# A mixture-of-experts, two-attention and quantised-FFN kernel: 39 whole expert tiles against 25 whole and 11 of two 64-row units

## What is computed

```python
gate = rmsnorm(x) @ wg_W + wg_b + (cond @ gg_W + gg_b)         # 8 experts
cw   = top-2 of softmax(gate), the other six zero
h1   = relu(x @ W1[e] + b1[e])                                 # 256 -> 512
h2   = relu(h1 @ W2[e] + b2[e])                                # 512 -> 512
m    = sum over e of cw[e] * (h2 @ W3[e] + b3[e])              # 512 -> 256
q, k, v = tanh(m @ W + b)                                      # 16 heads of 64
x1   = x + tanh(softmax_causal(q k^T / 8) v @ Wo + bo)
a    = attention of 16 heads of 16 on x1, its shares scaled by a gate and mixed with a field share
out  = x1 + quant(a) @ quant(ffn_weight)^T + bias              # blocks of 32, FP4 steps
```

## Time and profile before

| | us |
|---|---|
| median of three runs | 797.6 |
| the profiled execution, its own time | 797.88 |
| its span, first to last instruction | 796.0 |
| TensorE matmuls busy | 754.4 |
| VectorE busy | 497.0 |
| ScalarE busy | 279.1 |
| GpSimd busy | 81.4 |

### The profile page before, as it was taken

How to read it: one execution, slowest core, us unless ns; L and a number is a source line. 1 busy time by engine, 2 the same in 40 slices (tenths; PEclk the granted TensorE clock), 3 DMA queues, 4 the chain that set the end, 5 groups by cost and what they waited for, 6 DMA issues and landing times.

```text
span 796.0 us, 23085 instructions
## 1 busy us (share of the span) xinstructions
PE 754.4 (95%) x9468; PEld 656.8 (83%) x9468; DVE 497.0 (62%) x1090; ACT 279.1 (35%) x838; POOL 81.4 (10%) x91
## 2 busy tenths in 40 slices
PE   5489999999999999989999999999999999999786
PEld 2389989999999999967778878977897789778675
DVE  4764574443444454235688778777877787778756
ACT  3032112112212211244446435633563455336420
POOL 2221111111111100010000000000000000000000
PEclk9599999999999999999999999999999999999989
DMA  9788243111111112300000000010000000000000
GB/s 320 277 268 275 90 163 123 35 34 42 34 34 42 39 30 81 99 28 21 22 22 9 28 28 16 16 29 28 9 22 29 28 9 21 28 9 15 9 9 15
DMA packets 29686, 48.53 MB, mean 61 GB/s; under 512 B 3307, under 2 KB 19435, under 8 KB 29069
## 3 DMA queue, kind: packets, MB, share of 16 engines
q1 hardware_dynamic: 20432, 32.47, 12.0%
q0 software_dynamic: 3408, 9.31, 4.1%
q10 hardware_dynamic: 5741, 5.27, 2.0%
HBM read 39.82 MB, written 7.22 MB: 59 GB/s over the span
## 4 chain that ended last, share of the span: by engine, by line
PE 89%; DVE 7%; ACT 1%; issue 1%; another core or an unknown queue 1%; POOL 1%; DVEq 0%; ACTq 0%; POOLq 0%
PE ps L621 17%; PE ps L696 15%; PE ps L610 8%; PE ps L633 8%; PE ps L775 7%; PE ps L721 7%; PE ps L743 4%; PE ps L795 3%; PE ps L766 2%; PE ps L736 2%; PE ps L826 2%; PE ps L807 2%; PE ps L873 2%; PE ps L841 2%; PE ps L890 2%; PE ps L863 1%
## 5 line engine op out<-in xcount | busy, mean ns | idle before, releaser
L621 PE MATMUL ps<-h_t,w_now 128*128 128x128 f32 x1248 | 145.9, 275 | 1.0 <-DVE h_t L1362 1.0
L621 PEld LDWEIGHTS ps<-h_t,w_now 128*128 128x128 f32 x1248 | 142.4, 192 | 1.5 <-issue 1.4
L696 PE MATMUL ps<-arena,l_weights 128*128 128x128 f32 x1024 | 127.5, 279 | 3.0 <-ACT arena L1044 3.0
L696 PEld LDWEIGHTS ps<-arena,l_weights 128*128 128x128 f32 x1024 | 121.0, 194 | 4.3 <-ACT arena L1044 3.2
L1006 ACT ACTIVATE h_t<-ps,cols 128x128 f32<-128x128 f32 x156 | 44.5, 368 | 215.0 <-PE ps L610 193.7
L1353 DVE COPY w_now<-arena 128x2048 f32 x39 | 47.9, 1227 | 105.7 <-PE ps L621 98.8
L1050 ACT ACTIVATE arena<-ps,cols 128x128 f32<-128x128 f32 x256 | 73.1, 371 | 20.9 <-PE ps L696 20.9
L610 PEld LDWEIGHTS ps<-xg_t,w_now 128*128 128x128 f32 x624 | 75.3, 192 | 4.8 <-DVE w_now L1345 2.1
L610 PE MATMUL ps<-xg_t,w_now 128*128 128x128 f32 x624 | 76.4, 276 | 2.3 <-ACT xg_t L997 2.0
L633 PE MATMUL ps<-arena,h_t 128*128 x312 | 73.8, 379 | 0.0
L505 POOL DMA_INDIRECT xg<-in_x,slot_tok x39 | 45.7, 1173 | 232.8 <-PE ps L600 203.8
(11 more groups left out here) (245 smaller groups left out, 1011.9 us busy)
## 6 DMA issues: line engine op xcount, KB each, us to landing
arena<-in_w SPq DMA_DIRECT2D x16, 512.0 KB
arena<-in_w SPq DMA_DIRECT2D x8, 1024.0 KB
expert_out<-y ACTq DMA_DIRECT2D x39, 128.0 KB
arena<-in_x_t SPq DMA_DIRECT2D x2, 1024.0 KB, 6.4
arena<-in_x SPq DMA_DIRECT2D x16, 128.0 KB, 2.8
out<-arena SPq DMA_DIRECT2D x16, 128.0 KB, 1.7
b<-in_b SPq DMA_DIRECT2D x1, 1024.0 KB, 12.8
l_weights<-in_wq SPq DMA_DIRECT2D x1, 1024.0 KB
```

What stands on the lines that cost most here:

```text
L621: last = mm(ps[:, 2, m * P:(m + 1) * P], w2_now[:, k, m * P:(m + 1) * P], h1_t[j % 2][:, k, :], start=k == 0, stop=k == KM - 1)
L696: last = mm(ps[:, b, c * P:(c + 1) * P], wt[:, k, f:f + P], m_t[:, k, :], start=k == 0, stop=k == KH - 1)
```

## The change

- The 4096 rows are cut in 25 whole tiles of one expert and 11 **mixed** tiles of two units of 64 rows, each unit with an expert of its own: each expert's rows fill whole tiles as far as they go, and what is left goes into units. 36 tiles in all. The mixed ones run as positions 13 to 23 (FIRST_MIXED, LAST_MIXED).
- In a mixed tile the tokens are the stationary side (64 wide), one column half of TensorE for each unit, and the unit's W1, W2 or W3 streams 512 or 256 columns. The rows come out unturned: VectorE adds the bias rows (add_b1, add_b2; gathered by GpSimd, one row for each slot), TensorE turns them (turn_h1, turn_h2, four transposes each), ScalarE applies the ReLU. W1 and W2 are copied for both units (VectorE), W3 too (take_w3, ScalarE), which stands ahead of the store of y, now one step later than before in a mixed step.
- take_w1 and take_w2 wait for TensorE before they read the register, in all tiles.
- The dispatch computes three segments for each expert (first whole tile, other whole tiles, rest in units); independent instructions go out without a wait (step.go).
- The quantising of the FFN weight is spread over side stages j = 4 to 10, its transposes are at j = 8.
- SP loads the attention weights after layer 3 of position 23, since the second copies of the weights lie in that space.
- The values of token tile 0 lie in banks 1 and 2: l1_v(0) waits for no activation, the scores for the keys alone; keep_busy(12) is put behind l1_turn_m(1). VectorE mixes tile 1 before it adds the second half of tile 0's bias.

The diff, cut:

```diff
-SLOT_TILES = (TOPK * TOK + EXP * (P - 1)) // P
+UNIT = 64
+UNITS = P // UNIT
+FULL = -(-(TOPK * TOK - EXP * (P - 1)) // P)
+MIXED = -(-(TOPK * TOK - FULL * P + EXP * (UNIT - 1) - (UNIT - 1)) // P)
+SLOT_TILES = FULL + MIXED
 LAST = SLOT_TILES - 1
+FIRST_MIXED = EXP + 5
+LAST_MIXED = FIRST_MIXED + MIXED - 1
+BIAS_BUFS = 2
 H1, D1 = 16, 64
...
+def value_bank(t, s):
+
+    return (1, 2)[s] if t == 0 else (3, 0)[s]
...
+def mixed(p):
+
+    return FIRST_MIXED <= p <= LAST_MIXED
...
+def nth(p):
+
+    return p - FIRST_MIXED if mixed(p) else p if p < FIRST_MIXED else p - MIXED
...
+def slot_tile(p):
+
+    return FULL + nth(p) if mixed(p) else nth(p)
...
+    def go(self, instruction):
+        instruction.then_inc(self.sem, 1)
+        self.n += 1
...
+            sp.wait_ge(y_ps, LAST_MIXED + 1)
...
+                if mixed(j - 2):
+                    n = nth(j - 2)
+                    if n == 0:
+                        pool.wait_ge(row_expert_set, 1)
+                        pool.wait_ge(setup_done, 1)
+                        pool.wait_ge(fa_stored, 16)
+                    if n >= BIAS_BUFS:
+                        pool.wait_ge(h1r_set, n - BIAS_BUFS + 1)
+                    pool.indirect_dma_start(
+                        out=b1_rows[n % BIAS_BUFS], out_offset=None, in_=t_in["b1"],
+                        in_offset=bass.IndirectOffsetOnAxis(ap=row_expert[:, n:n + 1], axis=0)).then_inc(b1_gathered[n % BIAS_BUFS], 16)
...
-                    pool.wait_ge(y_stored, 16 * EXP)
+                    pool.wait_ge(y_stored, 16 * (LAST_MIXED + 1))
...
             def layer1(j):
-                pe.wait_ge(w1_set, j + 1)
                 pe.wait_ge(xt_set, j + 1)
                 if j:
-                    pe.wait_ge(h1t_set, j)
+                    if mixed(j - 1):
+                        pe.wait_ge(h1r_set, nth(j - 1) + 1)
+                    else:
+                        pe.wait_ge(h1t_set, j)
+                pe.wait_ge(w1_set, j + 1)
+                if mixed(j):
+                    for k in range(KH):
+                        for g in range(UNITS):
+                            part_ = slice(g * UNIT, (g + 1) * UNIT)
+                            last = mm(ps[part_, 0, :], xg_t[:, k, part_], w1_of[g][:, k, :],
+                                      start=k == 0, stop=k == KH - 1, tile_position=(0, g * UNIT))
+                    last.then_inc(l1_ps, 1)
+                    return
...
+            def turn_h1(j):
+                pe.wait_ge(h1r_set, nth(j) + 1)
+                if nth(j):
+                    pe.wait_ge(h1t_set, j)
+                for m in range(KM):
+                    last = pe.transpose(ps[:, 1, m * P:(m + 1) * P], h1_rows[:, m * P:(m + 1) * P], ident[:, :])
+                last.then_inc(h1r_turned, 1)
...
+                if mixed(j):
+                    pe.wait_ge(h2m_set, nth(j) + 1)
+                    pe.wait_ge(y_set, j)
+                    pe.wait_ge(w3_set, nth(j) + 1)
+                    for k in range(KM):
+                        for g in range(UNITS):
+                            part_ = slice(g * UNIT, (g + 1) * UNIT)
+                            last = mm(ps[part_, 4, 0:HID], h2_t[j % 2][:, k, part_], w3_now[g][:, k, :],
+                                      start=k == 0, stop=k == KM - 1, tile_position=(0, g * UNIT))
+                    last.then_inc(y_ps, 1)
...
                     layer1(j + 1)
                 if exists(j + 2, SLOT_TILES):
                     turn_x(j + 2)
+                if mixed(j - 1):
+                    turn_h2(j - 1)
                 if exists(j, SLOT_TILES):
                     layer2(j)
+                if mixed(j + 1):
+                    turn_h1(j + 1)
                 if exists(j - 1, SLOT_TILES):
                     layer3(j - 1)
 
...
-                if j == 7:
+                if j == 8:
...
-                pe.wait_ge(qk_set, 4 * t + 3 + s)
+                if t:
+                    pe.wait_ge(qk_set, 4 * t + 3 + s)
...
-                pe.wait_ge(vb_set, 2 * t + 2)
+                if t:
+                    pe.wait_ge(vb_set, 2 * t + 2)
+                else:
+                    pe.wait_ge(qk_set, 4)
...
             l1_turn_m(1)
+            keep_busy(12)
             l1_q(1, 0)
...
+            def relu2_mixed(j):
+                act.wait_ge(h2r_turned, nth(j) + 1)
+                act.wait_ge(y_ps, j - 1)
+                f(h2_t[j % 2][:, :, :], ps[:, 3, :].rearrange("p (k q) -> p k q", k=KM), ACT.Relu).then_inc(h2m_set, 1)
+
+            def take_w3(j):
+                if nth(j) == 0:
+                    act.wait_ge(setup_done, 1)
+                    act.wait_ge(fa_stored, 16)
+                    act.wait_ge(moe_loaded, 48 * EXP)
+                act.wait_ge(y_ps, j)
+                for g in range(UNITS):
+                    e = act.value_load(row_expert[g * UNIT:g * UNIT + 1, nth(j):nth(j) + 1], min_val=0, max_val=EXP - 1)
+                    at = act.snap(e * E_SIZE + W3_AT)
+                    last = act.copy(w3_now[g].rearrange("p k n -> p (k n)"), arena[:, bass.ds(at, KM * HID)])
+                last.then_inc(w3_set, 1)
...
+                if mixed(j - 1):
+                    take_w3(j - 1)
+                    if exists(j + 2, SLOT_TILES):
+                        copy_x(j + 2)
+                    relu2_mixed(j - 1)
+                    store_y(j - 2)
+                    if exists(j + 1, SLOT_TILES):
+                        relu1(j + 1)
+                else:
+                    if exists(j + 1, SLOT_TILES) and not mixed(j + 1):
+                        relu1(j + 1)
+                    if exists(j + 2, SLOT_TILES):
+                        copy_x(j + 2)
+                    if mixed(j + 1):
+                        relu1(j + 1)
+                if exists(j - 1, SLOT_TILES) and not mixed(j):
...
-            step(ts(first_slot, iota_m8, float(EXP), float(P), ALU.add, ALU.mult))
-            step(dve.memset(first_expert, 0.0))
-            step(ts(first_expert[:, 0:EXP], iota_m8[:, 0, :], float(EXP), None, ALU.add))
...
+            step.go(ts(full_i, count_i, -P, None, ALU.bitwise_and))
+            step(ts(up_i, count_i, float(UNIT - 1), None, ALU.add))
+            step.go(ts(seg_of[0], full_i, float(P), None, ALU.min))
+            step(ts(up_i, up_i, -UNIT, None, ALU.bitwise_and))
+            step.go(tt(seg_of[1], full_i, seg_of[0], ALU.subtract))
+            step(tt(seg_of[2], up_i, full_i, ALU.subtract))
+            step.go(dve.tensor_tensor_scan(seg_ends, seg, scan_zero.rearrange("p e i -> p (e i)")[:, 0:3 * EXP], 0.0, ALU.add, ALU.add))
+            step.go(tt(past_full, full_i, first_row, ALU.add))
...
             def take_w1(j):
+                if j:
+                    dve.wait_ge(l1_ps, j)
+                if mixed(j):
+                    if nth(j) == 0:
+                        dve.wait_ge(setup_done, 1)
+                        dve.wait_ge(fa_stored, 16)
+                        dve.wait_ge(moe_loaded, 48 * EXP)
+                    experts_of[j] = [unit_expert(j, g) for g in range(UNITS)]
+                    for g in range(UNITS):
+                        at = dve.snap(experts_of[j][g] * E_SIZE + W1_AT)
+                        last = dve.tensor_copy(w1_of[g][:, :, :].rearrange("p k n -> p (k n)"), arena[:, bass.ds(at, KH * MID)])
+                    last.then_inc(w1_set, 1)
+                    return
...
+            def take_w2(j):
                 if j:
-                    dve.wait_ge(l1_ps, j)
-                dve.tensor_copy(w1_now[:, :, :].rearrange("p k n -> p (k n)"), arena[:, bass.ds(at, KH * MID)]).then_inc(w1_set, 1)
-
-            def take_w2(j):
+                    dve.wait_ge(l2_ps, j)
+                if mixed(j):
+                    for g in range(UNITS):
+                        at = dve.snap(experts_of[j][g] * E_SIZE + W2_AT)
+                        last = dve.tensor_copy(w2_of[g][:, :, :].rearrange("p k n -> p (k n)"), arena[:, bass.ds(at, KM * MID)])
+                    last.then_inc(w2_set, 1)
...
+            def add_b1(j):
+                n = nth(j)
+                dve.wait_ge(l1_ps, j + 1)
+                dve.wait_ge(b1_gathered[n % BIAS_BUFS], 16 * (n // BIAS_BUFS + 1))
+                if n:
+                    dve.wait_ge(h1r_turned, n)
+                tt(h1_rows, bank(0), b1_rows[n % BIAS_BUFS], ALU.add).then_inc(h1r_set, 1)
...
+                if mixed(j + 1):
+                    add_b1(j + 1)
                 if exists(j + 2, SLOT_TILES):
                     take_w1(j + 2)
                 if j == LAST - 1:
                     l1_mix(0)
+                if mixed(j):
...
+                if j == 5:
+                    step(stt(xb(two(w_tmp)), xb(two(w_raw)), 1.0, bc(two(w_inv), BLK), ALU.mult, ALU.mult))
+                    step(ts(w_tmp, w_tmp, FP4_MAX, -FP4_MAX, ALU.min, ALU.max))
+                    step(ts(w_mag.bitcast(I32), w_tmp.bitcast(I32), EXPONENT, None, ALU.bitwise_and))
+                if j == 6:
```

(13 more changed lines are left out.)

225 lines of the change are left out of this document (158 added, 67 removed).

## The result

The changed kernel takes **787.65 us** (median of five runs, 786.08 to 789.31), the kernel before 797.6 (of its five runs beside them four lie between 795.66 and 798.33, one took 2634.36): ratio 0.987, 95% interval 0.985 to 0.989. The prediction was 789.0 us in a range of 782.0 to 796.5.

A forecast was written before the change was run, and what follows sets the result against it. TensorE, busy 95% of the span, bounds the kernel. Against the profiled 797.88 us: -21.9 + 13.8 + 1.0 + 1.0 + 1.2 - 1.6 - 0.9 - 1.4 = -8.8, giving 789.1, stated as 789.0 us; range 782 to 796.5.

The forecast's parts named there:

- Tiles out and mixed tiles in: Expert tiles: three steady steps fewer, -21.9 us; eleven mixed steps of 8.56 us, 1.26 above a full one, +13.8 us.
- Overlap and switching: Mixed-tile products: halves overlap at 0.427 us a pair pass; each visit to the 64-wide form costs about 0.31 us extra.
- (c): Mixed step: halves do not overlap because the stationary sides differ too; 15.4 us a step, 864 us in all; chance 4%.
- (d): Mixed steps: no switching cost and an early start of everything; 782 us in all; chance 10%.
- VectorE in the mixed step: VectorE's work, busy about 6.1 of 8.56 us, put at nothing while the mixed step stays above about 6.6 us.
- rival (b): Slower than before: VectorE bounds the mixed step, needing 9.6 us with all reads exposed; 801 us; chance 8%.
- Register reads: take_w1, take_w2: copies begin about 0.85 us later; 0.04 a full tile, +1.0 us, and first two tiles +1.0 us.
- rival (a): Full tiles: the register read becomes their bound, 0.3 us a tile, +7 instead of +1, 795 us; chance 12%.
- Dispatch: Path to the first x gather: new chain +2.0, three instructions gone -0.6, smaller tables -0.1; +1.2 us (0.5 to 2).
- Quantising: Tiles of 95.71 to 119.65: pieces hidden in VectorE's idle time remove TensorE's wait at L663; -1.6 us.
- The banks, the clock: Token tile 0: free banks start scores earlier, -0.9 us; keep_busy(12) shortens the idle piece, keeping the clock up, -1.4 us.

## Why the prediction was right

**Tiles out and mixed tiles in.** The step of 8.56 us came out as 8.57, eleven of them 13.9 above full tiles. The whole stretch costs 15.3 (124.88 us from the turn_x at 129.50 to that at 254.38, less 15 x 7.305): 13.9 are the eleven steps, 0.63 is the stall at the entry, the other 0.8 the edges, where a step has both forms (7.59, 8.63, 8.13 at the entry, 8.63, 7.95, 8.09 at the end). On the third chip, without the stall, it is 14.7. Neither was in the sum: VectorE and GpSimd had been put at nothing, and the edges were not looked at.

**Overlap and switching.** Both confirmed by their own runs: overlap whole only by alternation (11.25 us without it), 0.30 us a visit. Rivals (c) and (d) fall. The ground for (c), that the halves keep apart when the stationary sides differ too, is not borne out: they differ in every mixed step, and it takes 8.57 us. What costs overlap is the order of the products, and even with the halves in turn the step is 11.25 and the time 816, not 15.4 and 864.

**VectorE in the mixed step**, rival (b), needs 6.91 us, against 6.6 in the prediction and 9.6 in the rival; there were 1.66 us to spare.

**Register reads.** +1.0 at the start: 0.74. +1.0 for full tiles: nothing, and the whole of rival (a) with it. Slack and delay had been reckoned equal to 0.01, but the delay was mis-sized: 0.66 us in the full tiles, not 0.85, which leaves 0.31 ahead of the next layer 2. The 0.87 goes from the start of one copy to the start of the next, and 0.69 of it is the W1 copy itself. Full tiles stand 7.30 or 7.31 us apart with the read behind the wait as with the read ahead of it.

**Dispatch.** Predicted +1.2, made of +2.0 for the chain, -0.6 for three instructions and -0.1 for the tables. The chain took 6.78 us from 22.48 to 29.26 instead of 5.52: +1.26. The three instructions were 0.63 (17.23 to 17.86 in the trace of before) and the tables give 0.10, so the change's own part is **+0.5**: the chain was priced 0.7 too dear. That the stretch still came out at +2.24 is luck: of it 0.71 are the first tiles and 0.92 lie ahead of all new code, for VectorE's first instruction behind the gate's product begins at 15.71 in the trace of after and at 14.79 in that of before. This start scatters by 2.8 us over traces of the same code, which was not known.

**Quantising** -1.59, as predicted, and confirmed by its own run.

**The banks, the clock.** -0.85 to the scores, predicted -0.9 (its own rows, 343.11 - 342.3, give 0.8). The clock's 1.6 (predicted 1.4) was right in size, but **its cause is not shown to be the one named**: the prediction gave it to keep_busy(12) alone. The step that failed is the sentence "With keep_busy(12) ... the idle piece is about 1.8", which takes the piece as it was and fills it. The piece itself became shorter: 2.97 us before, 2.30 in the trace of after, 1.62 in the kernel without the products, since ScalarE starts 0.7 to 1.4 us sooner behind the scores. With the products and the old banks (2.93) the clock falls; without them and with the new banks (1.62) it stays. So they are neither enough nor, there, needed. Whether they were needed in the trace of after, where 2.30 would have stood idle, no run shows.

**Left out of the sum:** +0.4 ahead of the values of token tile 0 (0.32 of it a wait of layer 3 at 317.07 in after), and -0.4 behind the scores. There the exponentials start 2.43 us after the scores in the trace of after, 3.10 before and 3.06 with the old banks, 1.75 in two kernels of the first chip and 1.22 to 1.36 in the others, with the same products ahead. What delays ScalarE there stays open.

So the errors were +1.5 (edges and stall), -1.0 (reads of full tiles), +0.4 ahead of the values and -0.6 behind the scores, and within the start -0.7 (dispatch) and -0.3 (first reads) against +0.9 of scatter. They cancel, and that is luck: the total was off by 0.4 of 8.8 us in the span, single terms by more. The median fell by 10.0 us, the profiled executions by 8.6. What was right without luck is the mechanism that carries the time: three tiles out, and mixed tiles at 8.57 us.

## What to carry to other kernels

A step of a pipeline that TensorE bounds can be costed from rows of the same form elsewhere in the kernel: passes of a pair at 0.427 us, 0.30 us a visit and 0.11 us a transpose gave 8.56 where 8.57 came. Read an idle weight load against the matmul beside it before calling it a loss, and cost the edges of a new stretch as well as its steady step. Where two edits sit at one place and one of them is meant to cure an effect, work out the effect with the other alone, and when a run takes one out, see in its rows that nothing else moved: here ScalarE did.
